# Loading the next layer's weights in eleven parts over eight turns of the stream, in place of five transfers at one place of the layer

## What is computed

```python
def attn_layer(x, Wqkv, qs, ksc, Wo):
    qkv = x @ Wqkv                         # 128 -> 3 x 1024
    q, k, v = split and reshape to 16 heads of 64
    q = l2norm(q) * qs; k = l2norm(k) * ksc
    q, k = rotary(q), rotary(k)
    out = local_attention(q, k, v)         # windows of 32, looking one window back
    return out @ Wo                        # 1024 -> 128

def ffn_layer(x, g, bln, W1, b1, W2, b2):
    xn = layernorm(x) * g + bln
    a, gate = split(xn @ W1 + b1)          # 2 x 341
    return a * gelu(gate) @ W2 + b2

for i in range(6):
    x = attn_layer(shift_tokens(x), ...) + x
    x = ffn_layer(shift_tokens(x), ...) + x
```

## Time and profile before

| | us |
|---|---|
| median of 3 runs | 1903.02 |
| profiled execution, its own time | 1892.94 |
| its span (first to last instruction) | 1891.0 |
| PE (TensorE matmul) busy | 1757.0 (93%) |
| DVE (VectorE) busy | 1536.1 (81%) |
| POOL (GpSimd) busy | 1235.3 (65%) |
| ACT (ScalarE) busy | 1152.6 (61%) |

### The profile page before, as it was taken

One profiled execution on the slowest core, in us unless ns is written; L12 is line 12 of the kernel. 1 busy time (PEld: TensorE's weight loads), 2 busy tenths in 40 slices (PEclk: granted clock), 3 DMA queues, 4 the chain that ended last, 5 costly groups with the idle time before them and its releaser, 6 DMA issues.

```text
span 1891.0 us, 72845 instructions
## 1 busy us (share of the span) xinstructions
PE 1757.0 (93%) x31224; PEld 1190.0 (63%) x31224; DVE 1536.1 (81%) x2117; ACT 1152.6 (61%) x2221; POOL 1235.3 (65%) x789
## 2 busy tenths in 40 slices
PE   7699977899999999999899999999998999999985
PEld 2255653667666667676666666676766776667663
DVE  6599857898889878888688887889887888888863
ACT  5533224576767666767567676667675767576752
POOL 3477735776767666777567676677676777677740
PEclk9799978999999999999899999999999999999997
DMA  4545002222222332322322223222223322232220
GB/s 98 129 59 75 2 3 82 78 71 70 70 67 72 100 83 61 80 65 75 116 70 70 69 70 116 75 68 72 70 73 105 81 60 79 58 80 63 77 66 26
DMA packets 68257, 137.28 MB, mean 73 GB/s; under 512 B 17952, under 2 KB 23520, under 8 KB 66912
## 3 DMA queue, kind: packets, MB, share of 16 engines
q1 hardware_dynamic: 67936, 132.62, 27.3%
HBM read 29.79 MB, written 2.10 MB: 17 GB/s over the span
## 4 chain that ended last, share of the span: by engine, by line
PE 77%; issue 5%; DVE 4%; DMA 3%; POOL 3%; SPq 3%; ACT 1%; DVEq 0%; POOLq 0%; ACTq 0%
PE bank L1375 15%; PE bank L1448 10%; PE bank L1388 9%; PE bank L1465 9%; PE bank L1380 8%; PE bank L1423 8%; PE bank L1482 7%; PE bank L1506 3%; PE bank L1410 2%; DVE ff_T L1827 1%; PE bank L1472 1%; SPq L1251 1%; DMA p_T<-p_blocks 1%; DMA v_rep<-v_by_step 1%; PE bank L1476 1%
## 5 line engine op out<-in xcount | busy, mean ns | idle before, releaser
L1775 DVE TENSOR_TENSOR rot<-bank,gains 128x1024 f32<-128x1024 f32 x384 | 466.8, 1217 | 121.7 <-ACT squares L1608 115.1
L1319 POOL TENSOR_TENSOR rot<-rot,rnorm 128x1024 f32<-128x1024 f32 x192 | 361.0, 1901 | 312.5 <-ACT rnorm L1618 305.9
L1313 POOL TENSOR_TENSOR rot<-rot 128x1024 f32<-128x1024 f32 x192 | 455.2, 2371 | 74.3 <-DVE rot L1775 74.3
L1375 PE MATMUL bank<-wqkv,x 128*128 128x512 f32 x768 | 398.9, 613 | 8.0 <-DVE rot L1775 3.3
L1608 ACT ACTIVATE squares<-bank 128x512 f32<-128x512 f32 x384 | 230.1, 599 | 258.9 <-PE bank L1375 251.9
L1649 ACT ACTIVATE o_T<-bank 128x512 f32<-128x512 f32 x192 | 104.2, 598 | 226.8 <-PE bank L1448 226.8
L1337 POOL TENSOR_TENSOR probs<-probs,total 128x1024 f32<-128x1024 f32 x96 | 182.6, 1902 | 76.6 <-DVE total L1803 76.3
L1781 DVE TENSOR_REDUCE rnorm<-squares 128x16 f32<-128x1024 f32 x192 | 227.7, 1186 | 0.2 <-issue 0.2
L1448 PEld LDWEIGHTS bank<-p_T,v_shift 64*64 64x64 f32 x6144 | 169.1, 138 | 77.3 <-issue 69.8
L1448 PE MATMUL bank<-p_T,v_shift 64*64 64x32 f32 x6144 | 194.3, 223 | 23.6 <-DMA p_T<-p_blocks 20.6
L1388 PE MATMUL bank<-st_ident,rot 128*128 128x128 f32 x1536 | 205.3, 277 | 2.9 <-issue 2.0
(11 more groups left out here) (198 smaller groups left out, 2853.3 us busy)
## 6 DMA issues: line engine op xcount, KB each, us to landing
p_T<-p_blocks SPq DMA_DIRECT2D x768, 64.0 KB
v_shift<-v_tok SPq DMA_DIRECT2D x96, 384.0 KB, 3.5
v_shift<-v_tok SPq DMA_DIRECT2D x96, 128.0 KB, 3.4
wqkv<-in_wqkv SPq DMA_DIRECT2D x6, 1536.0 KB, 7.9
v_rep_sb<-v_by_step SPq DMA_DIRECT2D x32, 128.0 KB
v_rep<-v_by_step SPq DMA_DIRECT2D x32, 128.0 KB
wo<-in_wo SPq DMA_DIRECT2D x6, 512.0 KB, 8.7
w<-in_w SPq DMA_DIRECT2D x6, 341.0 KB, 8.8
```

Source lines behind the costliest of these rows:

```text
L1313: nc.gpsimd.tensor_tensor(out=out, in0=out, in1=halves_of, op=ALU.add).then_inc(rot_added.sem, 1)
L1319: nc.gpsimd.tensor_tensor(out=by_head(qk[u][:, half]), in0=by_head(qk[u][:, half]), in1=rnorm[u][:, AH * i:AH * (i + 1)].unsqueeze(2).to_b ...
L1375: nc.tensor.matmul(QK_BANKS[i][:, :], shifted_tokens(x, n, P), layer_cols(wqkv, n, 3 * INNER, 512 * i, 512), start=True, stop=True).then_i ...
L1775: nc.vector.tensor_tensor(both, src.unsqueeze(1).to_broadcast([P, 2, 8, DH]), pair_of_gains.unsqueeze(2).to_broadcast([P, 2, 8, DH]), ALU. ...
```

## The change

The layer's weights become a list of eleven parts: wqkv in six parts of 512 columns (256 KB each), qk_gain (128 KB), wo in two parts of 512 columns (256 KB each), w1 (341 KB) and w2 (192 KB). `load_part` issues one of them. In each of layers 0 to 4, after `place(n)` for n = 6 to 13, SP issues the parts i of the next layer with i * 8 // 11 == n - 6. That is two wqkv parts after n = 6, one after 7, two after 8, one after 9, qk_gain after 10, the two wo parts after 11, w1 after 12 and w2 after 13. The load of layer 1, before at the start of the stream, is now spread over layer 0 in the same way. Layer 0 is still loaded in `load_early`, in one place, but in eleven transfers instead of five. `w_loaded` counts eleven transfers a layer.

```diff
+LAYER_PARTS = (("wqkv", 0, 512), ("wqkv", 512, 1024), ("wqkv", 1024, 1536), ("wqkv", 1536, 2048), ("wqkv", 2048, 2560), ("wqkv", 2560, 3072),
+               ("qk_gain", 0, 4 * DH), ("wo", 0, 512), ("wo", 512, 1024), ("w1", 0, 2 * FF), ("w2", 0, len(FF_PARTS) * C))
+LOAD_TURNS = 8
...
-    LAYER_LOADS = 5
+    LAYER_LOADS = len(LAYER_PARTS)
...
-    def load_layer(sp, layer, slot):
-        for tile, name, width in ((wqkv, "wqkv", 3 * INNER), (wo, "wo", INNER), (w1, "w1", 2 * FF), (w2, "w2", len(FF_PARTS) * C)):
-            sp.dma_start(tile[slot][:, :], a[name][ds(layer, 1), :, :].rearrange("l p n -> p (l n)")).then_inc(w_loaded.sem, 16)
-        sp.dma_start(qk_gain[slot][:, :], a["qk_gain"][ds(layer, 1), :].to_broadcast([P, 4 * DH])).then_inc(w_loaded.sem, 16)
+    def load_part(sp, layer, name, c0, c1):
+
+        tile = {"wqkv": wqkv, "wo": wo, "w1": w1, "w2": w2, "qk_gain": qk_gain}[name][layer % 2]
+        if name == "qk_gain":
+            sp.dma_start(tile[:, :], a[name][ds(layer, 1), :].to_broadcast([P, c1])).then_inc(w_loaded.sem, 16)
+        else:
+            sp.dma_start(tile[:, c0:c1], a[name][ds(layer, 1), :, c0:c1].rearrange("l p n -> p (l n)")).then_inc(w_loaded.sem, 16)
...
-        load_layer(sp, 0, 0)
+        for part in LAYER_PARTS:
+            load_part(sp, 0, *part)
...
-        load_layer(sp, 1, 1)
-        EARLY = 7
-        for n in range(BLOCKS):
-            place(n)
-        for layer in range(1, DEPTH - 1):
-            for n in range(EARLY):
+        EARLY = 6
+        for layer in range(DEPTH - 1):
+            for n in range(BLOCKS):
                 place(layer * BLOCKS + n)
-            sp.wait_ge(x_ready.sem, x_ready.after(layer * BLOCK_PAIRS - 1))
-            sp.wait_ge(w_loaded.sem, w_loaded.after(layer))
-            load_layer(sp, layer + 1, (layer + 1) % 2)
-            for n in range(EARLY, BLOCKS):
-                place(layer * BLOCKS + n)
+                if n == EARLY and layer:
+                    sp.wait_ge(x_ready.sem, x_ready.after(layer * BLOCK_PAIRS - 1))
+                    sp.wait_ge(w_loaded.sem, w_loaded.after(layer))
+                for i, part in enumerate(LAYER_PARTS):
+                    if i * LOAD_TURNS // LAYER_LOADS == n - EARLY:
+                        load_part(sp, layer + 1, *part)
```

## The result

The changed kernel takes 1871.51 us, the median of 4 executions (1863.99 to 1872.72); the kernel before, beside it, 1902.61 (1900.36 to 1903.59). The ratio is 0.9836, with a 95% interval of 0.9814 to 0.9858: 31 us faster. The prediction was 1873.6, in a range of 1867 to 1888.

The account below looks back on a forecast made before the run. TensorE was taken to bound the kernel, standing still in four long pairs of turns. Removing 33.4 us, adding 3 for tight turns and 1 for issue stops gave -29.4: from 1903.0 to 1873.6 us, range 1867 to 1888.

Parts of the forecast that it names:

- What the change removes: TensorE's four long pairs of turns at the loads of layers 2 to 5: 33.4 us, the gain's upper bound.
- What it adds: Parts in 20 even-n turns of layers 0 to 4 cost 3 us; TensorE's issue stops cost 1 us.
- The absorption of the backlog: 1.3 us of weights ahead of p_T is largely worked off while p_T's eight transfers are still being issued.
- The slack of a tight turn: In even-n turns, p_T issued 1.80 us behind v, `outputs` leaves at most 1.45 us, estimated 0.7 usable.
- the 0.7 I had given as the sign: Sign of being right: in even-n turns p_T's issue behind v's starts at most 0.7 us later.
- Edits taken at nothing: Layer 1's moved load, wait places, last part and six more issues in `load_early` cost 0; the last up to 2 us.
- The sum for the profiled execution: The profiled execution of the whole kernel would go from 1892.94 to 1863.5 us, by -29.4 us.
- I carry the difference over: The runs' median lies 10.1 us above the profiled execution; this was kept for the changed kernel, giving 1873.6 us.
- The issue stops of the kernel before: Rival: TensorE's stops of 3.58 and 3.07 us within score matmuls recur, giving 1883 us; chance 0.12.
- The tight turns lose: Rival: 20 even-n turns lose half the 1.3 us bound, 1884 us, or all of it, 1897; chance 0.08.
- The clock did fall in tight turns: Rival: at `outputs` in 20 even-n turns, waits plus slower clock cost 49 us, giving 1919; chance 0.03.
- Every transfer having a price of its own: Rival: each part holds SP's queue until landing, six more in five layers costing 105 us, giving 1975; chance 0.01.

Follow-up runs that it names:

- e2: Changed kernel with all eleven parts of a layer behind place(6) and layer 1 loaded at the start of the stream: 1901.4 us, ratio 1.0008.
- e7: Kernel before with one number changed, the whole five-transfer load behind place(7) instead of place(6): 1872.3 us, ratio 0.9847.
- e0: The changed kernel run once more with no edit: 1868.8 us, ratio 0.9845 to the kernel before.
- f1: The changed kernel again, no edit, in more rounds: 1870.4 us, ratio 0.9837 to the kernel before.
- e4: Changed kernel with the parts issued in turns of even n only, three after n = 6, 8 and 10, two after 12: 1872.1 us, ratio 0.9853.
- e6: Changed kernel with five whole transfers over five turns instead of eleven parts, wqkv after n = 6: 1889.5 us, ratio 0.9943.
- f4: Changed kernel with layers 0 and 1 loaded whole, then only six and five 16-column transfers after n = 6 and 8: 1885.0 us, ratio 0.9898.
- e1: Changed kernel with layer 1 loaded before the turns and nothing loaded for layers 2 to 5, the floor: 1867.3 us, ratio 0.9823, stream 1476.0.
- e5: Changed kernel with six parts issued after n = 6 and the other five after n = 8: 1902.0 us, ratio 0.9997.
- f3: Changed kernel with all eleven parts of a layer behind place(7), layers 1 to 5: 1878.6 us, ratio 0.9899.

## Why the prediction was right, point by point

**What the change removes** (33.4 us, as the excess of four pairs over an ordinary one): right. The pairs lost 31.9 us. The trace after has one wait of 0.2 us for p_T in the stream, and e2 and e7 show the cause from both sides: the same bytes stall TensorE behind place(6), whether in five transfers or eleven, and hardly do so behind place(7).

What those 33.4 us were made of, the prediction did not split. The windows of the ordinary pair and of the four long ones of the kernel before do:

```profile
619.65:650.62 30.97, 30.86 (x615) 21.62 (x617) 27.16 (x34) 21.49 (x41) 22.38 (x14) 1.00 0.27 70
650.62:690.62 40.00, 34.38 (x614) 23.07 (x617) 27.18 (x34) 21.83 (x41) 22.42 (x14) 0.91 0.41 124
910.36:950.73 40.37, 34.33 (x615) 24.30 (x617) 27.17 (x34) 21.87 (x41) 22.37 (x14) 0.87 0.41 123
1168.14:1206.21 38.07, 33.79 (x615) 22.90 (x616) 27.27 (x34) 21.65 (x41) 22.44 (x14) 0.91 0.43 130
1424.95:1463.81 38.86, 33.25 (x615) 23.95 (x616) 27.18 (x34) 21.81 (x41) 22.34 (x14) 0.91 0.42 128
```

For the same matmuls TensorE is busy 12.3 us longer than in four ordinary pairs, at a clock of 0.87 to 0.91: more than a third of the loss is the slow clock behind the stops. The other 21.1 us are the stops. Only the second and the fourth pair have a long wait for p_T, 5.93 and 5.50 us; in the first and the third the stops are issue stops, behind which p_T's delay is hidden (e2 above). The two long waits, from TensorE's timeline:

```profile
929.26 0.44 PE L1448 MATMUL bank<-p_T,v_shift 64*64 64x32 f32 x8 [5.93 <-DMA p_T<-p_blocks]
...
1443.42 0.44 PE L1448 MATMUL bank<-p_T,v_shift 64*64 64x32 f32 x8 [5.50 <-DMA p_T<-p_blocks]
```

One reading of the prediction is wrong in a detail: not all of rows 3 lies in the long pairs. Its fourth wait, 2.07 us, is at the start of the stream, and the changed kernel still has it (2.04 us).

**What it adds** (3 us in the tight turns and 1 in issue stops): the stream gained 28.2 us, 3.7 less than the four pairs, where 4 less were forecast. But e0 and f1 have 1476.3 and 1476.1 against the floor of 1476.0. The 4 us need not be a cost of the parts: it is near what the stream varies by (2.9 us between two profiles of one kernel). By two profiles of three the term is nearer 0, by the first it is 3; it was mis-sized, if at all, upwards.

**The absorption of the backlog**, by which 1.3 us of data ahead of p_T costs nothing, held for the size that the change has, and e4 shows it nearly holding at three parts. As a rule it was wrong: from the same working I expected at most 0.8 us for 3.9 us of data in e6 and found up to 3.38. The step that failed there is that weights and p_T alike move at 394 GB/s. While both were on the way the engines moved 231 to 313, and with mostly p_T left 118 at a share of 0.66, which would be 179 if they were full (an estimate from that row).

**The slack of a tight turn** (at most 1.45 us, 0.7 usable) is not measured by itself. It fits: in e4 p_T goes out 0.7 us late in most turns with three parts, up to 1.4 in single ones, and the waits are at most 0.9 us; in f4 it is some 2 us late (2.7 in the turn shown), and the waits are up to 1.9. In the changed kernel p_T's issue starts 1.6 to 2.6 us behind v's in tight turns, so at most 0.8 us late, about the 0.7 I had given as the sign.

**Edits taken at nothing.** In `load_early` SP was later at the recurrence's copies, 76.98 against 73.44 us, and GpSimd read them without a wait. The timelines of SP and POOL of the changed kernel:

```profile
76.98 10.33 SPq L453 DMA_DIRECT2D v_rep<-v_by_step  x16
```

```profile
112.47 1.28 POOL L832 TENSOR_TENSOR v_rep<-v_rep,k_sb 128x512 f32<-128x512 f32 x1
```

112.47 is 0.56 later than 111.91, as is this whole phase in this execution; its first ACT row after 66 us is 0.57 later too, ahead of the load. The later start of the stream in this execution (342.78) does not come from here either, as e0 has the same edits and starts at 338.66.

**The sum for the profiled execution** (1863.5) missed by 8.6 us, and the median (1873.6) only by 2.1. The step that failed is "I carry the difference over". The 10.1 us between the profiled execution of before and the median is no constant of the program. Two profiles of the changed kernel differ by 11.9, mostly by the clock in the recurrence's end (0.55 against 0.69 in the window from 240 to 260 us) and in the tail. The forecast of the median was right because it took the stream's gain from the median itself. There is some luck in how close it came: the gain by the medians is 31 to 32 us (after, e0, f1) against 29.4, and that the stream of 1507.4 us holds for the executions of 1903 us too rests on one profile of the kernel before. It is plausible: with the later start (4.1) and the slower tail (4.9) between the two profiles of the changed kernel, its 1892.9 would be 1901.9, an estimate.

**The rivals.** The issue stops of the kernel before were neither a cost of their own nor gone for good: e2 lost them and was no faster. The tight turns lose next to nothing in the changed kernel, though they would with six parts. The clock did fall in tight turns, behind some waits for p_T of 1.7 us and more in e6 and f4 (0.50 behind 3.38 and 1.92 us, 0.61 behind 1.73), but not behind all: it stayed at 1.00 in the 3.4 us behind one of 2.33. In the changed kernel there was no such stop for p_T. Every transfer having a price of its own is refuted by e0 against e1: 44 transfers more, 0.3 us in the stream.

## What to carry to other kernels

Before splitting or spreading a bulk transfer, look at what stands behind it in its queue in that very turn, and at that work's slack: here moving the load by one turn, one changed number, gained as much by the medians as spreading it, and by the stream most of it (23 of 28 to 31 us). If it must go where the slack is small, its issuing should fit the queue's idle time and its data should be well under what was seen to hurt (two parts of 256 KB cost little or nothing, three some 6 us in all, six were as bad as the whole). Compare stages of a trace, not whole executions, where the clock of other stages differs by more than the effect.

## What the runs showed of the hardware that I had not expected

- A stop of 1 to 2 us on TensorE can be followed by 3.4 us at half clock: 1.92 us in f4 was, and 0.94 us in e5. It need not be: the changed kernel has issue stops of up to 1.8 us in its stream, and the clock behind that one was 1.00, as it was in its four pairs. In 3.4 us at half clock 1.7 us of work are lost, so a short wait can cost two to three times its length.
- TensorE stops for "issue" in the middle of runs of matmuls, 15.7 us in e1 with no weights on the way in that stretch, and up to 5.0 us a time where a backlog fills the DMA engines (e5, f3).
- The same program's tail of 200 matmuls took 43 or 48 us, with a granted clock of 0.74 or 0.61.
- 1536 KB in one transfer ahead of the eight of p_T made TensorE wait 1.4 to 3.4 us in all five turns (e6), though the eight were issued over 5.99 us in the turn shown and the 1536 KB alone would take 4 us at 394 GB/s. The engines did not reach that rate with both on the way (231 to 313).
